# The q/k/v convolution of a pair of windows moved from four to five steps ahead of its scores, and the row work by one step

## The reference

```python
xn = group_norm(x)                                   # 32 groups: each channel by itself
xw = windows(xn)                                     # 4*64 windows of 32 x 16 x 16
q, k, v = [shuffle_invert(conv3(xw, w, b), 2) for ...]   # 128 features x 64 tokens
q, k, v = [layer_norm(t.T, g, b) for ...]            # over the 128 features
attn = softmax(q @ k.T * hd**-0.5 + rel_bias)        # 8 heads of 16 features, 64 x 64
out = pixel_shuffle((attn @ v) @ proj_w.T + proj_b, 2)
xr = image(xw + out)
y = xr + conv3(gelu(conv3(xr, c1w, c1b)), c2w, c2b)
return x + y
```

## Time and profile before

| | |
|---|---|
| median of 3 runs | 833.27 us (832.16 to 835.34) |
| profiled execution | 835.37 us |
| its span | 833.5 us |
| PE busy | 753.8 us, 90% of the span |
| PE weight loads | 538.0 us, 65% |
| DVE busy | 656.3 us, 79% |
| ACT busy | 603.4 us, 72% |
| POOL busy | 491.1 us, 59% |
| mean granted TensorE clock | 0.988 of full speed |

### The profile page before, as it was taken

One profiled execution on the slowest core, in us unless ns is written; L12 is line 12 of the kernel. 1 busy time (PEld: TensorE's weight loads), 2 busy tenths in 40 slices (PEclk: granted clock), 3 DMA queues, 4 the chain that ended last, 5 costly groups with the idle time before them and its releaser, 6 DMA issues.

```text
span 833.5 us, 18393 instructions
## 1 busy us (share of the span) xinstructions
PE 753.8 (90%) x5704; PEld 538.0 (65%) x5704; DVE 656.3 (79%) x2141; ACT 603.4 (72%) x1287; POOL 491.1 (59%) x1041
## 2 busy tenths in 40 slices
PE   0479999989899999999899999998989999999988
PEld 0347777767456777777556677776745677776753
DVE  6548888879768888888757888887877888887575
ACT  1488888876577888876747888877757788887750
POOL 5447776763356777765246776776235677776410
PEclk9989999999999999999899999999999999999999
DMA  7101160000112142100111216100011303000002
GB/s 255 57 29 29 31 230 22 36 2 1 58 64 94 31 135 96 58 2 1 58 39 52 70 30 230 57 2 1 2 57 64 96 30 130 0 1 1 2 1 101
DMA packets 17643, 47.00 MB, mean 56 GB/s; under 512 B 2080, under 2 KB 2720, under 8 KB 17568
## 3 DMA queue, kind: packets, MB, share of 16 engines
q1 hardware_dynamic: 17568, 46.09, 16.1%
HBM read 37.69 MB, written 8.39 MB: 55 GB/s over the span
## 4 chain that ended last, share of the span: by engine, by line
PE 47%; DVE 18%; issue 12%; ACT 11%; POOL 10%; DVEq 0%; DMA 0%; SPq 0%; ACTq 0%; POOLq 0%
PE y_ps L1013 12%; PE o_bank L1092 5%; PE s_ps L1067 4%; PE pt_ps L1080 4%; POOL ln_rs L724 4%; DVE ln_st L542 3%; ACT qk_n L858 3%; PE s_ps L1126 3%; PE ox_ps L1036 3%; PE ox_ps L1126 3%; PE o_bank L1126 3%; PE pt_ps L1126 3%; DVE pt L584 2%; PE t_ps L1047 2%; ACT sc L873 2%
## 5 line engine op out<-in xcount | busy, mean ns | idle before, releaser
L858 ACT ACTIVATE qk_n<-y_ps,ln_nr,ln_rs 128x128 f32<-128x128 f32 x256 | 103.7, 459 | 84.7 <-POOL ln_nr L727 84.0
L737 POOL TENSOR_TENSOR sc<-sc,mx 128x512 f32<-128x512 f32 x128 | 133.7, 1045 | 37.8 <-DVE mx L577 37.4
L1013 PE MATMUL y_ps<-w_hi,x_hi 128*128 128x192 f16 (+1 forms) x512 | 150.1, 293 | 0.0
L1013 PE MATMUL y_ps<-w_lo,x_hi 128*128 128x192 f16 (+1 forms) x512 | 149.6, 292 | 0.0
L1013 PE MATMUL y_ps<-w_hi,x_lo 128*128 128x192 f16 (+1 forms) x512 | 149.5, 292 | 0.0
L1092 PE MATMUL o_bank<-v_bd,pt 128*128 128x66 f32 x1024 | 128.6, 268 | 0.0
L562 DVE TENSOR_TENSOR sc<-s_ps,biasS 128x512 f32<-128x512 f32 x128 | 86.8, 678 | 50.3 <-PE s_ps L1067 49.0
L542 DVE BATCH_NORM_STATS2 ln_st<-y_ps 128x6 f32<-128x128 f32 x384 | 88.9, 287 | 45.6 <-PE y_ps L1013 43.9
L1092 PEld LDWEIGHTS o_bank<-v_bd,pt 128*128 128x128 f32 x1024 | 124.5, 192 | 0.2
L724 POOL TENSOR_TENSOR ln_rs<-ln_ve,neg_half 128x3 f32<-128x3 f32 x128 | 113.0, 883 | 10.7
L873 ACT ACTIVATE sc<-sc 128x512 f32<-128x512 f32 x128 | 81.5, 636 | 39.4 <-POOL sc L737 39.3
(11 more groups left out here) (181 smaller groups left out, 1614.6 us busy)
## 6 DMA issues: line engine op xcount, KB each, us to landing
xs<-in_x_sh_dram SPq DMA_DIRECT2D x32, 576.0 KB, 4.2
xst<-in_x_al_dram SPq DMA_DIRECT2D x16, 512.0 KB, 8.0
xf<-in_x_al_dram SPq DMA_DIRECT2D x32, 256.0 KB, 5.4
out_dram<-xf SPq DMA_DIRECT2D x32, 256.0 KB, 2.0
wst<-in_wqkv_dram SPq DMA_DIRECT2D x1, 768.0 KB, 4.1
w1s<-in_w_dram SPq DMA_DIRECT2D x1, 256.0 KB, 8.7
w2s<-in_w_dram SPq DMA_DIRECT2D x1, 256.0 KB, 8.7
biasS<-in_bias_t_dram SPq DMA_DIRECT2D x1, 256.0 KB, 9.5
```

The lines of the kernel that those rows point to most:

```text
L737: pool.tensor_tensor(sc[i % 4][:, :, :, :], sc[i % 4][:, :, :, :], mx[i % 2][:, :, :].unsqueeze(2).to_broadcast([P, HP, TOK, 2]), ALU.subt ...
L858: ins = act.activation(qk_n[j][:, t, :].rearrange("p (h y x) -> p h y x", h=HEADS, y=2), by_head(y_ps[j][:, E * t:E * (t + 1)]), ACT.Identity,
L1013: ins = pe.matmul(y.rearrange("p (t e) -> p t e", t=3)[:, :, cols], xx[r % 2][:, s, a % 2, 2 * TS * (a // 2):2 * TS * (a // 2 + TS)], ww[: ...
```

## The change

Everything that makes q, k and v of a pair is asked for one step earlier, counted from its scores: convolution, statistics, scales, `qk_n` and `v_bd` of step `i` are those of pair `i + 5`. The transposes of q and k stay those of pair `i + 3`. An image gets one step more at its start, -5, and the last convolution stands in step 26. The c2 tiles of the image before, two in step -4 until now, are spread over steps -5 and -4. The row's memsets and normalisation go from the steps with `i % 4 == 3` to those with `i % 4 == 1` before them, its high halves to `i % 4` of 3 and 0, its low halves to 0 and 1: two steps earlier for the first, one step for the others.

```diff
--- before.py
+++ after.py
@@ -232,7 +232,7 @@
         stored = sem("stored")
         ADD0 = 1
         BODY, BODIES = 8, 2
-        HEAD = range(-4, 4)
+        HEAD = range(-5, 4)
         EPILOGUE = range(HEAD.stop + BODY * BODIES, PAIRS + 4)
 
         c_ps = [y_ps[0][:, :], y_ps[1][:, :], s_ps[:, 0, :], s_ps[:, 1, :]]
@@ -267,8 +267,8 @@
         pt_bank = pt_ps[:, :, :].rearrange("p h n -> p (h n)")
         c2_bank = [c_ps[3], c_ps[2], pt_bank, o_bank[:, :], ox_ps[:, :], pt_bank, o_bank[:, :], ox_ps[:, :]]
 
-        c2_in = {-4: (0, 1), -3: (2,), -2: (3,), -1: (4,), 0: (5,), 1: (6,), 2: (7,)}
-        result_in = {-3: (0, 1), -2: (2,), -1: (3,), 0: (4,), 1: (5,), 2: (6,), 3: (7,)}
+        c2_in = {-5: (0,), -4: (1,), -3: (2,), -2: (3,), -1: (4,), 0: (5,), 1: (6,), 2: (7,)}
+        result_in = {-4: (0,), -3: (1,), -2: (2,), -1: (3,), 0: (4,), 1: (5,), 2: (6,), 3: (7,)}
         start_in = {-2: 0, -1: 1, 2: 2, 3: 3}
         bias_in = {21: 0, 23: 1, 25: 2, 27: 3, 29: 4, 31: 5, 33: 6, 34: 7}
         stats_in = {27: (0,), 28: (1, 2), 29: (3, 4), 30: (5, 6, 7)}
@@ -533,8 +533,8 @@
                     for r in range(2):
                         row(r, (b + 1) * NROW)
 
-                if has(i + 4):
-                    m = i + 4
+                if has(i + 5):
+                    m = i + 5
                     v.wait_ge(conv_done, p0 + (m + 1))
                     if m >= 2:
                         v.wait_ge(ln_scales, p0 + (m - 1))
@@ -546,7 +546,7 @@
                     for t in range(3):
                         ins = v.bn_aggr(ln_mv[m % 2][:, t, :], ln_st[m % 2][:, t, :])
                     ins.then_inc(ln_moments, 1)
-                if last is not None and i == -4:
+                if last is not None and i == HEAD.start:
                     for t in range(BORDER1, T1N):
                         low(last, t)
                     border(last, T1N, 2)
@@ -583,8 +583,8 @@
                         v.wait_ge(pv_done, p0 + (m - 1))
                     v.tensor_copy(pt[m % 2][:, :, :], pt_ps[:, :, :]).then_inc(pt_copied, 1)
 
-                if i % 4 == 3 and 2 <= (i + 9) // 4 < NROW:
-                    row((i + 9) // 4, r0)
+                if i % 4 == 1 and 2 <= (i + 11) // 4 < NROW:
+                    row((i + 11) // 4, r0)
 
                 if has(i - 2):
                     m = i - 2
@@ -738,7 +738,7 @@
                                        mx[i % 2][:, :, :].unsqueeze(2).to_broadcast([P, HP, TOK, 2]),
                                        ALU.subtract).then_inc(shifted, 1)
                 if 2 <= (i + 8) // 4 < NROW:
-                    for z in ((), (0,), (1,), ())[i % 4]:
+                    for z in ((0,), (1,), (), ())[i % 4]:
                         low((i + 8) // 4, z, p0, r0)
                 for r in split_in.get(i, ()):
                     split(b, r)
@@ -815,10 +815,10 @@
 
             def step(i, p0, h0, r0, rr0, row0, b=None, followed=False, last=None):
 
-                if i % 4 == 3 and 2 <= (i + 9) // 4 < NROW:
-                    row((i + 9) // 4, r0, rr0)
-                if 2 <= (i + 8) // 4 < NROW and i % 4 < 2:
-                    high((i + 8) // 4, i % 4, p0, r0)
+                if i % 4 == 1 and 2 <= (i + 11) // 4 < NROW:
+                    row((i + 11) // 4, r0, rr0)
+                if 2 <= (i + 9) // 4 < NROW and (i + 1) % 4 < 2:
+                    high((i + 9) // 4, (i + 1) % 4, p0, r0)
 
                 if i % 2 == 0 and has(i + 2):
                     h = (i + 2) // 2
@@ -1017,7 +1017,7 @@
                     ins.then_inc(conv_done, 1)
 
                 if last is not None:
-                    if i == -4:
+                    if i == HEAD.start:
                         c1(last, 11)
                         c1(last, 12)
                     for t in c2_in.get(i, ()):
```

## The result

The changed kernel takes **840.81 us** (median of 15 runs, 836.1 to 845.6 and one of 889.96) against 833.48 us for the kernel before, measured beside it: ratio 1.0083, 95% interval 1.0062 to 1.0103. The run of 889.96 us, at a mean granted clock of 0.844, stands apart from the other 14 and is left out of the ratio and of what follows; the median of the 14 is 839.8 us. The kernel is slower by more than the 0.5% that a measurement can tell. The forecast was 836.0 us, no change; the time lies inside the range of 825 to 841 by 0.2 us, on the side to which a chance of 0.25 was given.

What follows compares the result with a forecast made beforehand. PE was taken as the fullest engine, its waits hanging on ACT's chain behind DVE's memsets. Terms -8.3 + 1.2 - 4.0 + 10.4 + 0 + 3.4 = +2.7 us on 833.27 gave 836.0 us, range 825 to 841.

Steps and rivals of the forecast that it cites:

- Steps 9, 13, 17, 21: Loop steps shrink from 4.66 to 4.14 us as memsets leave the front of DVE's statistics: -8.3 us.
- Step 23: The projection waits longer for ACT's copy `ot`, 0.3 us in each of four images: +1.2 us.
- Steps 26 to 28: Convolution taken from step 27 leaves PE idle, not won; step 28's transposes lose their 0.99 us wait: -4.0 us.
- Boundaries: Three image boundaries: an added convolution, 1.64 us, and a wait for `v_bd` of pair 0, 1.8 us: +10.4 us.
- Filling: Fill of the first image: waits pass from `qk_n` to `v_bd` and the exponential; 0, between -1 and +1.5 us.
- The clock: PE's 2.8 us idle in step 27 may drop its clock; half a drop per image: +3.4 us, 0 to 6.8.
- rival 2: The clock falls in step 27 of every image, costing as much as after 217: 839.4 us, chance 0.18.
- Rival 1: All 19.9 us of the q/k transposes' waits go, none returns at the exponential: 823.8 us, chance 0.15.
- rival 3: Row work only moved: DVE late in steps 5, 9, 13, 17 instead, 8.3 us not won: 844.3, chance 0.07.

Runs made afterwards that it cites:

- the row work alone: The kernel before with only the row's memsets and normalisation moved to steps with i % 4 == 1, convolution still four ahead: 824.28 us, ratio 0.9899.
- the lead alone: The changed kernel with the row's memsets, normalisation, high and low halves back at their former steps: 975.98 us, ratio 1.1685.
- the short run: First profiled execution of the changed kernel, nothing altered, one of its shortest: 836.53 us.
- the median run: A later profiled execution of the changed kernel, nothing altered, almost exactly at its median: 840.96 us.
- the longest run: A further profiled execution of the changed kernel, nothing altered: 847.66 us.

## Why the prediction was right, and where not

- **Steps 9, 13, 17, 21** (-8.3): right in size and cause. The table has -8.05 and -7.90, the row work alone -8.4, and the lead alone leaves step 13 at 4.86.
- **Step 23** (+1.2): +1.0.
- **Steps 26 to 28**: the convolution taken out was not won, as forecast: without a fall of the clock the stretch to the first c1 tile is 18.66 against 18.69. Step 28's -4.0 came as -4.6 in the short run. The cause, the split in front of pair 31's normalisation, is borne out by the run with the split behind it; but pair 31 a step earlier isn't needed, as the run with the last convolution in step 27 shows.
- **Boundaries** (+10.4): +9.95 in the short run, and the wait for `v_bd` is where it was put. In the median run +12.5: 1.4 us more in two of the three, where the clock stayed at half longer.
- **Filling** (0, -1 to +1.5): this step failed. It came out at -0.5 in the short runs and **+2.4 in the median run**, and the clock is not the reason. The -0.5 compares a filling without a fall of the clock with one that had two. With two in both, the kernel before took 35.19 and the median run 37.62; with none in either, the row work alone took 31.30 and the short run 34.68. So the longer lead costs the filling 2.4 to 3.4 us at an equal clock. The waits went from `qk_n` to `v_bd` as forecast; which of them holds the extra time, no run takes apart.
- **The clock** (+3.4, 0 to 6.8): mis-sized, and put in the wrong places. It was priced in step 27 alone, with one length of stretch, and as half a fall an image. Over four profiles of the changed kernel the idle was followed by a fall 11 times in 16, at two prices: 1.45 us an image in the first profile, and 20.24 + 3.19 - 18.66 - 1.69 = 3.1 in the first image of the longest run. In the median run only one step 27 had a fall, 20.02 + 3.26 - 18.67 - 1.69 = 2.9 us, less than the 3.4 put down; the longer stretches behind the boundaries came on top. The Trainium skill (TensorE: Matmul & The Clock Gate, "What's actually happening") ties the gate to how busy PE has recently been; the two runs with other work in the idle of step 27 agree (a fall in one image of four, and in none), and the prediction's reading of it, that each of these idles brings a fall, held 11 times in 16.

The profile of the median run is 5.6 us longer than that of the kernel before, where the sum was +2.7: the filling is 2.4 above its term, the boundaries 2.1, and the rest together 1.6 below. That the median still lies inside the range, by 0.2 us, is luck: the range was drawn to reach over rival 2, and not for a longer filling.

**Rival 2** has the direction, slower by the clock, but not the place. It asked for a fall in step 27 of every image; the four profiles have three, four, three and, in the median run, one. That the idle there matters for the median is shown by the run with the last convolution in step 27; a longer filling stood in no rival. Its price of 839.4 was close by luck, and its chance of 0.18 too low. Rival 1 is ruled out by the wait at the exponential and by the lead alone, rival 3 by the row work alone. What stays open is why one execution of the same program gets the shorter and another the longer stretches. The same section of the Trainium skill says that the same kernel is slow at its start for a different number of matmuls from run to run, by where the gate's own period stands; the runs show a spread behind idles inside the kernel, and none tests whether that is its cause.

## What to carry to other kernels

Split a change into its parts before judging it: here one half was worth -1.0% and the other cost more than that, and the half that helped was a row's memsets and normalisation, with the memsets in front of a chain that three engines wait for. Work taken out in front of a wait that another engine ends isn't won; it becomes idle time, and on PE idle time has a second price behind it. Where a kernel's runs suddenly spread, profile a long one as well as a short one before explaining the median, and compare a stretch with the same stretch before only where the clock fell as often in both.

## What the runs showed that was not expected

The same program, on the same chip, ran between 836.1 and 847.7 us with its loop the same to 0.1%: behind the same idle of 2.75 us the granted clock stayed at 1.00 in five of 16 cases and fell to half for a shorter or a longer stretch in the others. Read in stretches of 0.5 us, the seven short ones began within 0.5 us of the start of the projection and lasted 3.4 us, the four long ones began 1.2 to 1.7 us behind it and lasted 6.8. Shorter idles were followed by a fall too: 1.64 us in step 31 of three images, 1.59 us in step 26 of one image of four, with the last convolution back in step 27 (of two images in the run with the c2 tiles moved as well).
